# Row transposes in two pairs with a core tile or the gates between them, in a fused cross-attention and mixture-of-experts kernel

## What is computed

```
h = x @ down_w + down_b                       # 512 -> 256
logits = x @ router_w + router_b - 1e-7 * cost  # 8 experts
gate = softmax(top_k(softmax(logits), 2))
for each of the 2 choices, for each expert e (hidden 256, 512, 768 or 1024):
    acc += gelu(gelu(h * mask_e) @ w1_e + b1_e) @ w2_e + b2_e      # times gate
out += 0.1 * (gelu(gelu(h) @ shared_w1 + shared_b1) @ shared_w2 + shared_b2)
out = out @ up_w + up_b + gelu(x) @ core_w + core_b
```

## Time and profile before

| | |
|---|---|
| median of the runs | 732.62 us (732.62 to 734.15) |
| profiled execution | 740.14 us, its span 738.0 us |
| TensorE busy | 687.9 us, 93% of the span |
| ScalarE busy | 541.0 us, 73% |
| VectorE busy | 525.0 us, 71% |
| GpSimd busy | 480.7 us, 65% |
| DMA | 123.98 MB, mean 168 GB/s |
| mean granted clock of TensorE | 0.995 |

### The profile page before, as it was taken

How to read it: one execution, slowest core, us unless ns; L and a number is a source line. 1 busy time by engine, 2 the same in 40 slices (tenths; PEclk the granted TensorE clock), 3 DMA queues, 4 the chain that set the end, 5 groups by cost and what they waited for, 6 DMA issues and landing times.

```text
span 738.0 us, 20869 instructions
## 1 busy us (share of the span) xinstructions
PE 687.9 (93%) x6101; PEld 373.1 (51%) x6101; DVE 525.0 (71%) x853; ACT 541.0 (73%) x1129; POOL 480.7 (65%) x474
## 2 busy tenths in 40 slices
PE   1799998999999999999989999799999999999988
PEld 0122222232333333322355544588888888888744
DVE  3989998899999999998877756544444444444456
ACT  2399999899999999999885665487676666767411
POOL 3558788888888898985477244046666666656623
PEclk9999999999999999999999999999999999999999
DMA  6656666656655666545255635599988888887487
GB/s 201 199 151 196 199 207 217 197 175 208 209 192 186 208 207 220 177 139 182 93 166 182 210 118 175 147 172 174 126 119 121 118 135 106 108 102 94 56 250 277
DMA packets 136865, 123.98 MB, mean 168 GB/s; under 512 B 70612, under 2 KB 106196, under 8 KB 136792
## 3 DMA queue, kind: packets, MB, share of 16 engines
q1 hardware_dynamic: 121928, 106.58, 50.4%
q0 software_dynamic: 13632, 15.47, 14.7%
q10 hardware_dynamic: 1232, 0.98, 0.5%
HBM read 60.33 MB, written 51.53 MB: 152 GB/s over the span
## 4 chain that ended last, share of the span: by engine, by line
PE 71%; DVE 10%; DMA 7%; issue 5%; ACT 3%; SPq 3%; POOL 1%; ACTq 0%; DVEq 0%; POOLq 0%
PE EH L1295 25%; PE Y L1295 16%; PE pv L561 12%; PE ring L548 8%; DVE mx L707 6%; PE nat L536 5%; ACT P L632 2%; DMA k_scratch<-khl 1%; DMA QS<-mrow 1%; DVE statx L688 1%; PE ring L580 1%; DMA q_scratch<-qhl 1%; SPq L396 1%; PE ring L571 1%; DMA y_sums<-ysb,to 1%
## 5 line engine op out<-in xcount | busy, mean ns | idle before, releaser
L707 DVE TENSOR_REDUCE mx<-nat 128x2 f32<-128x1024 f32 x256 | 296.8, 1213 | 23.2 <-PE nat L536 22.3
L632 ACT ACTIVATE P<-ring 128x512 f32<-128x512 f32 x512 | 279.4, 603 | 19.8 <-PE ring L548 9.8
L2091 POOL DMA_INDIRECT y_sums<-ysb,to x84 | 138.4, 1647 | 101.6 <-DVE ysb L2028 88.5
L561 PE MATMUL pv<-P,VT 128*32 128x256 f32 x2048 | 158.7, 394 | 0.4
L536 PE MATMUL nat<-KS,QS 48*128 48x512 f16 x512 | 111.8, 397 | 24.4 <-DMA QS<-q_scratch 15.1
L548 PE MATMUL ring<-QS,KS 49*128 49x512 f16 x512 | 123.5, 392 | 9.1 <-ACT P L632 8.5
L1641 ACT ACTIVATE X<-EH,bcur 128x256 f32<-128x256 f32 x168 | 85.6, 559 | 50.9 <-DVE u L1992 27.0
L1295 PE MATMUL Y<-whi,u 128*128 x672 | 117.1, 273 | 0.5 <-DVE u L1992 0.5
L1295 PE MATMUL EH<-XA,whi 128*128 128x256 f16 x672 | 116.9, 273 | 0.3 <-DMA XA<-g_rows 0.3
L1992 DVE TENSOR_TENSOR u<-X,u 128x512 f16<-128x512 f32 x84 | 57.7, 687 | 78.3 <-ACT u L1647 76.5
L1295 PE MATMUL Y<-wlo,u 128*128 x336 | 91.6, 273 | 0.0
(11 more groups left out here) (266 smaller groups left out, 995.4 us busy)
## 6 DMA issues: line engine op xcount, KB each, us to landing
XA<-in_wall SPq DMA_DIRECT2D x8, 800.0 KB, 4.4
u<-in_wall SPq DMA_DIRECT2D x8, 800.0 KB, 4.4
QS<-q_scratch SPq DMA_DIRECT2D x64, 96.0 KB, 2.5
KS<-k_scratch SPq DMA_DIRECT2D x62, 96.0 KB, 2.2
X<-in_x SPq DMA_DIRECT2D x16, 256.0 KB, 2.8
q_scratch<-qhl SPq DMA_DIRECT2D x16, 256.0 KB, 2.1
xr<-in_x SPq DMA_DIRECT2D x16, 256.0 KB, 3.7
rd<-den_scratch SPq DMA_DIRECT2D x16, 256.0 KB
```

The costliest lines, as they stand in the source:

```text
L561: m = pe.matmul(pv[32 * j:32 * j + 32, q], VT[i][:, lb, g, j, :], Pb[4 * (s % 2) + j][:, q], start=(lb == 0 and half == 0), stop=(lb == 3) ...
L632: act.activation(Pb[4 * (s % 2) + j][:, :], bank[:, :], ACT.Exp).then_inc(t_use.sem, 1)
L707: dve.tensor_reduce(mx[:, k // 8, :, k % 8], nat[k % 2][:, :, :], AX.X, ALU.max).then_inc(t_max.sem, 1)
L2091: pool.indirect_dma_start(out=ysum[:, :], out_offset=bass.IndirectOffsetOnAxis(ap=to[:, j % 2, a:a + 1], axis=0), in_=ysb[j % 2][:, a, :], ...
```

## The change

The change is in the tables of `seq` and in two places that follow them.

- TensorE, body 0: the four `rt` are split in two pairs, and the two extra products and `gt` stand between the pairs.
- TensorE, bodies 1 and 2: behind the first pair comes `core` 1 of the body before, then `gt`, then the second pair. In body 3: `core` 0 of the body before stands between the pairs, and `gt` comes behind the second.
- ScalarE, body 0: `guh` 0 and 1 come before the rows; `gt` stands between rows 0, 1 and rows 2, 3. The copy of `zs` is tied to `guh` 1 instead of `gu` 3, that of `Zs` to `row` 1 instead of `row` 3.
- ScalarE, bodies 1 and 2: `gt` stands between rows 0, 1 and rows 2, 3. Body 3 keeps its order.
- VectorE, GpSimd and SyncE keep their order. One line is added to the file, so that line numbers behind 1018 grow by one in the changed kernel.

```diff
@@ seq, body 0
-                "pe": four("uT") + [("lg", 0), ("lt", 0), ("h", 0), ("h", 1), ("rk", 0)] + four("rt") + [("gt", 0)],
...
+                "pe": four("uT") + [("lg", 0), ("lt", 0), ("h", 0), ("h", 1), ("rk", 0), ("rt", 0), ("rt", 1), ("gt", 0), ("rt", 2), ("rt", 3)],
...
@@ seq, pe
-                (old([("y", 0)]) + cur(four("rt")) + old([("core", 0)]) if last else old([("y", 0), ("core", 0)]) + cur(four("rt"))) + \
-                cur([("gt", 0)]) + old([("core", 1), ("core", 2)])
+                (old([("y", 0)]) + cur([("rt", 0), ("rt", 1)]) + old([("core", 0)]) + cur([("rt", 2), ("rt", 3), ("gt", 0)]) + old([("core", 1)]) if last else
+                 old([("y", 0), ("core", 0)]) + cur([("rt", 0), ("rt", 1)]) + old([("core", 1)]) + cur([("gt", 0), ("rt", 2), ("rt", 3)])) + \
+                old([("core", 2)])
@@ scalar, rest
-                    if o == (0, "gu", 3):
+                    if o == (0, "guh", 1):
                         act.wait_ge(t_z.sem, 4)
...
-                    elif o == (0, "row", 3):
+                    elif o == (0, "row", 1):
                         act.wait_ge(t_z.sem, 6)
```

More of the change, by code:

```diff
@@ L1004, in seq @@
             return [(0, *o) for o in {
-                "pe": four("uT") + [("lg", 0), ("lt", 0), ("h", 0), ("h", 1), ("rk", 0)] + four("rt") + [("gt", 0)],
-                "act": [("pexp", 1), ("h", 0), ("gh", 0), ("e2", 0), ("gu", 0), ("gu", 1), ("h", 1), ("gh", 1), ("gu", 2), ("gu", 3)] +
-                       four("row") + [("gt", 0)] + four("guh"),
+                "pe": four("uT") + [("lg", 0), ("lt", 0), ("h", 0), ("h", 1), ("rk", 0), ("rt", 0), ("rt", 1), ("gt", 0), ("rt", 2), ("rt", 3)],
+                "act": [("pexp", 1), ("h", 0), ("gh", 0), ("e2", 0), ("gu", 0), ("gu", 1), ("h", 1), ("gh", 1), ("gu", 2), ("gu", 3), ("guh", 0), ("guh", 1)] +
+                       [("row", 0), ("row", 1), ("gt", 0), ("row", 2), ("row", 3), ("guh", 2), ("guh", 3)],
                 "dve": four("uf") + [("lpc", 0)] + four("ul") + R_(["lred", "lb", "lmx", "lsub", "lcl"] + route_a + route_s + route_p) +
@@ L1024, in seq @@
                 old([("a", 1), ("sah", 1)]) + older([("acc", 0), ("acc", 1)]) + cur([("pexp", 1), ("h", 0), ("gh", 0), ("h", 1), ("gh", 1), ("e2", 0)] + ([("nz", 0)] if last else [])) + \
-                cur(four("row") + [("gt", 0)] + four("gu"))
+                cur((four("row") + [("gt", 0)] if last else [("row", 0), ("row", 1), ("gt", 0), ("row", 2), ("row", 3)]) + four("gu"))
             if last:
```

## The result

The change takes 728.2 us (median of 9 runs, 725.99 to 730.75), before takes 732.92 us beside it (9 runs, 731.43 to 734.35). The ratio is 0.9936, with a 95% interval of 0.9922 to 0.9949: **4.7 us faster** (3.7 to 5.7). Forecast were 727.7 us and a gain of 4.9. The profiled execution of the change is its third shortest, 727.5 us with a span of 725.4.

A forecast was written before the change was run, and what follows sets the result against it. TensorE was taken as the bound: no idle time in the expert loop, holes in the four bodies before it. Body 0's 2.3 us plus 2.64 us from bodies 1 to 3 gave 4.9 us off 732.62: 727.7 us, range 726.4 to 730.6.

The forecast's parts named there:

- The pairs in bodies 1 to 3: TensorE's row transposes: a core tile between the pairs removes the wait for ScalarE's row copies, 0.88 us per body, 2.64 us.
- The reading of core 1 behind `gtl`: VectorE, bodies 1 to 3: core tile 1 is read later, with 3.4 us of slack before its bank's next use: no cost.
- Body 0, TensorE and VectorE: Early guh and gt shorten the chain to the fourth uT and rk of body 1: 3.0 us against the profile, 2.3 without a clock fall.
- The contention: VectorE, body 0: gul 2, 3 took 2.37 us beside GpSimd's tensor_tensor and would take 1.3 when run before 382.2.
- Rival A: TensorE's clock falls in body 0 after the change too, behind two 0.8 us holes: gain 3.2 us, 729.4 us; chance 0.21.
- The sum: Whole kernel: 2.3 + 2.64 = 4.9 us off the 732.62 us median, giving 727.7 us; 5.6 us against the profiled execution.
- the step from 3.0 to 2.3 us: Body 0: the median taken as a run without a clock fall there, so only 2.3 of 3.0 us are gained.
- Rival B: The first block's load, not TensorE, sets the experts' start: about 3.2 us gained (729.4) or nothing (732.6); chance 0.12.
- Rival C: Core tile 1 signalled 5.84 us late in bodies 1 to 3, against 3.4 us of slack: slower, 736.6 us; chance 0.05.
- the late signal: Last body: VectorE got core tile 1 5.84 us late, unexplained; it may belong to the profiled execution.
- the 7.5 us of excess: Profiled execution's 740.14 us against the 732.62 us median of runs; part of it may belong to that execution.
- The forecast of 0.89 for faster: Whole kernel: probability 0.89 of being faster by over 0.2% (1.5 us); same 0.06, slower 0.05.

The follow-up runs named there:

- e3: The kernel before with only guh 0, 1 of body 0 ahead of zs and the rows on ScalarE: 740.24 us, ratio 0.9995 to before.
- e4: The kernel before with only the pairs of body 0 split around bias products and gt, guh still behind the rows: 740.09 us, ratio 0.9984 to before.
- c2: The kernel before, unchanged, run for its profile on another chip: its own single run 741.95 us; before's median there 741.45 us.
- g1: f1 again, timed in rounds on a chip where before takes 733.33 us: 729.41 us, ratio 0.9946 to before.
- g2: f1 with the last four scatters of body 3 also held until VectorE has read core tile (2,1): 729.89 us, ratio 0.9957 to before.
- f1: The change with GpSimd's scatters of bodies 1 and 2 held until VectorE has read the previous body's last core tile: 736.67 us, one run; before 742.19 there.
- c1: The change once more, on another chip where before takes 741.45 us: 739.24 us, ratio 0.9987 to before.
- e1: The kernel before with only the change's body 0 part, bodies 1 to 3 as before: 742.31 us, ratio 1.0026 to before.
- e2: The kernel before with only the change's part in bodies 1 to 3, body 0 as before: 742.56 us, ratio 1.0029 to before.
- f3: The change with VectorE making all tables of the last body ahead of reading core tile (2,1): 738.59 us, ratio 0.9947 to before.

## Why the prediction was right, and where only half

**The pairs in bodies 1 to 3** (forecast 0.88 us per body). rk 1 to 2 took 26.84 us in the profile of before, with no late tile in that body, and takes 25.94 now: 0.90. From rk 2 on, every profile of before that I have has late tiles, so the 0.88 of bodies 2 and 3 can't be read off alone; that rk 2 to 3 takes 25.95 in the changed kernel as well is as forecast. The reading of core 1 behind `gtl` held up nothing, as costed, and rows 2 and 3 of the scatters stayed hidden.

**Body 0, TensorE and VectorE** (forecast: fourth `uT` 2.05 us earlier, holes of 0.8 and 0.75, `rk` at 390.3). Measured, on the old clock: 2.13 us, holes of 0.67 and 0.56, `rk` at 390.47. The piece shrank by 2.85 us where 3.0 were forecast against the profile. `gul` came out at 1.29 us. The contention moved on: the last two `ul` took 3.10 us beside GpSimd's last norm, where the first two took 1.28, so `ul` ended at 385.2 (386.0 on the old clock) instead of 385.0. The statistics, which were to wait for GpSimd until 385.75, started behind `ul` at 385.15 (385.91), 0.2 us later. zs starts at 375.28 on the old clock, inside the 375.4 asked for. By e3 and e4 nearly all of it is the early `guh`.

**The clock.** Rival A is refuted: 1.00 with holes of 0.67 and 0.56 us, and in the other profiles with `guh` ahead. The Trainium skill (TensorE: Matmul & The Clock Gate, section What's actually happening) says that activity releases the throttle; the shorter holes without a fall agree. Still, the reason given against this rival was weak. It was that the clock hadn't fallen over 470 to 474 us of before, with TensorE busy for 1.36 us of four. In c2, the same kernel, it fell at that place (0.78 over the same stretch, TensorE busy for 1.87 us of the four before 472), as in six others of the eleven profiles, and the falls in the attention stand behind holes of 1.0 us. That it didn't fall behind 0.67 and 0.56 us could not be told from that row.

**The sum.** 2.3 + 2.64 = 4.9 was forecast against the median and 4.7 measured, with 3.7 to 5.7 as its interval. Whether before's clock falls in body 0 on the result's chip as it does on the others isn't shown, since no profile of before was taken on that kind; 4.9 and 5.5 (2.85 and three times 0.9) both lie in the interval. So the step from 3.0 to 2.3 us, which rests on three runs, two of them equal, is neither confirmed nor refuted.

**Rival B.** TensorE starts the experts 0.24 us behind the start of its last y product, where its y products stand 0.11 us apart: at most 0.13 us can be the load's. The two do move together, as forecast.

**Rival C and the late signal: the step that was only half right.** The prediction took the late tile, "which I can't explain", and part of the 7.5 us of excess for what may be the profiled execution's own. The excess goes with the chip: on three chips the median of before is 741 to 742 us, in the result's runs and on the chip of g1 and g2 it is 733, no run of before under 738.17 us was seen on the first three, and none over 734.96 in the others. It isn't the clock: at a mean granted clock of 1.000 before took 738.17 us on the chip of f1 and 730.97 on that of g1. Each chip was used on one occasion only, so that the chip can't be told from the occasion. The arithmetic nearly closes: on the 733 kind, rk 2 to 3 and the end of before should take 26.84 and, with 0.9 for the pairs, 21.83 + 0.9 = 22.7 us; in the profile they took 28.44 and 27.25, 6.2 us more, of the 7.5. (The two 0.9 are the changed kernel's, since no profile of before was taken there; and the 0.76 us in front of body 0 can't be counted, as its `rk` starts anywhere from 372.5 to 376.7 in the fourteen profiles.) Rival C had the right cause and the wrong tile. It asked for 4.6 us on core tile 1, with 3.4 us of slack, and that tile is on time in bodies 1 and 2 of the change. The late one is tile 3, 2.57 us in c1, whose bank TensorE wants back for the fourth `uT`: there the slack is 0.5 us, and 2.06 us are waited. That is too little to make the change slower; but the late updates do take what it brings: e1 and e2, each half of it, are not faster than before, and the whole is at 0.9987. The forecast of 0.89 for faster is a forecast for the kind of chip that the medians came from, and the result was timed on that kind. That it wasn't timed where the profile came from is luck: the prediction didn't ask. There "same" fits better (0.9987, 0.996 to 1.0014).

Open: which holds which. The scatters' own updates are thinned out far more: from 420 to 470 us their four semaphores have 51 to 110 recorded updates on the 741 kind and 250 to 272 on the other. Open too is why some chips don't show it, and what of the 741 us is left when no update is late. f1 shows, in one run, that the late updates follow the scatters in time; it doesn't show the mechanism, and the variant with fewer scatters wasn't tried, since the blocks would then be read from rows that nobody wrote.

## What to carry to other kernels

If the profile's own time is 1% above the median of the runs, ask where it comes from before taking it for noise: profile the same kernel once more where the medians were taken, and write the forecast against that profile. A consumer that reads a tile microseconds after the producer's last instruction, and a releaser that lies behind that tile in the producer's order, are the sign of a late counter. Keep short work that others depend on from standing behind the tile in that consumer's queue (f3, 3.2 us up to E0 in one profile). Starting indirect scatters behind a chain of semaphores instead of beside it may be worth trying (f1, one run); no timed gain of either over the change is shown.

## What the runs showed of the hardware that I had not expected

Chips (or occasions) differ by 1.1 to 1.3% on this kernel: 732.9 and 733.3 us against 741.1, 741.5 and 742.2. On the slower ones TensorE's semaphore updates reach VectorE up to 6.5 us late and in bursts, while GpSimd's indirect scatters are under way or up to 1.7 us behind their last updates. TensorE is held in part, too: 0.7 to 2.3 us ahead of the last burst, with some matmuls 0.7 us apart, besides what it waits for late readers. Behind such waits the granted clock falls between 400 and 476 us in eight of the eleven profiles, which costs 1.4 us more (28.67 against 27.25 us). The scatters themselves aren't slower to issue, 0.96 us in both kinds.

Two subtractions of VectorE with both operands in SBUF (`ul`) took 1.28 us and the next two 3.10 us beside GpSimd's tensor_tensor of the norm, but weren't slowed beside its indirect DMAs (`gul`, 1.29 us for two). Part of the spread of the runs of one kernel, 3 to 11 us, goes with the mean granted clock: on the chip of g1 and g2, before took 730.97 us in the run at 1.000 and 734.96 in the one at 0.993, 4.0 us for 0.7% of some 730, which is 5.1 us of the clock's time. These are two runs; the others scatter around that line.
